# Context products moved into the attention stage, a first tile turned early, and fewer barriers in a two-layer decoder kernel

## What is computed

```
k = concat(context, x) ; q = x @ wq ; scores = q . (k @ wk) / sqrt(D)
out = softmax(scores) @ (concat(context, x) @ wv) @ wo
```

## Time and profile before

| what | us |
|---|---|
| median of 3 runs | 2226.31 (2226.2 to 2229.31) |
| the profiled execution's own time | 2224.11 |
| its span in the trace | 2222.4 |
| PE busy | 2093.0 (94%) |
| DVE busy | 1250.0 (56%) |
| POOL busy | 541.8 (24%) |
| ACT busy | 516.3 (23%) |

### The profile page before, as it was taken

One profiled execution on the slowest core, in us unless ns is written; L12 is line 12 of the kernel. 1 busy time (PEld: TensorE's weight loads), 2 busy tenths in 40 slices (PEclk: granted clock), 3 DMA queues, 4 the chain that ended last, 5 costly groups with the idle time before them and its releaser, 6 DMA issues. The chain is left out here.

```text
span 2222.4 us, 29341 instructions
## 1 busy us (share of the span) xinstructions
PE 2093.0 (94%) x11935; PEld 1221.2 (55%) x11935; DVE 1250.0 (56%) x1825; ACT 516.3 (23%) x783; POOL 541.8 (24%) x511
## 2 busy tenths in 40 slices
PE   7899999878999899899999898999999999999996
PEld 5444444324444466556665565566666666666654
DVE  2467777666999944022222225365757585847466
ACT  1444444440000121111111121122222222222121
POOL 2122222226777400011111221112121212111111
PEclk9999999989999999999999999999999999999998
DMA  8950000005111145521212412101010101000000
GB/s 171 99 48 29 29 29 20 31 10 200 46 42 42 34 140 190 200 67 62 67 67 67 178 40 96 48 1 48 1 58 1 58 1 39 1 29 11 1 10 20
DMA packets 65649, 129.57 MB, mean 58 GB/s; under 512 B 6416, under 2 KB 19856, under 8 KB 65520
## 3 DMA queue, kind: packets, MB, share of 16 engines
q1 hardware_dynamic: 44864, 75.39, 13.3%
q10 hardware_dynamic: 14976, 33.69, 4.2%
q0 software_dynamic: 5680, 18.62, 2.8%
HBM read 96.36 MB, written 41.81 MB: 62 GB/s over the span
## 5 line engine op out<-in xcount | busy, mean ns | idle before, releaser
L937 PE MATMUL conv_conv<-kv,toep 128*128 128x512 f32 x576 | 248.5, 594 | 0.0
L2434 DVE RECIPROCAL tail_inv<-tail_ring 128x256 f32<-128x256 f32 x64 | 112.4, 1756 | 188.7 <-PE tail_ring L1772 181.4
L1456 PE MATMUL moe_gu_ps<-gu,moe_xT 128*128 x624 | 199.0, 462 | 3.9 <-issue 2.3
L937 PEld LDWEIGHTS conv_conv<-kv,toep 128*128 128x128 f32 x576 | 110.0, 191 | 139.0 <-issue 131.6
L960 POOL TENSOR_TENSOR kv<-vT,cT 128x512 f32<-128x512 f32 x128 | 147.2, 1172 | 58.1 <-PE conv_conv L937 53.6
L1456 PEld LDWEIGHTS moe_gu_ps<-gu,moe_xT 128*128 128x128 f32 x624 | 116.0, 191 | 73.0 <-issue 23.6
L2125 POOL TENSOR_TENSOR tail_rstd_x<-tail_rstd_x,const_minus_half 128x2 f32<-128x2 f32 x31 | 21.9, 707 | 499.0 <-DVE tail_rstd_x L2386 499.0
L2132 POOL TENSOR_SCALAR_AFFINE_SELECT tail_expT<-tail_expT 128x1024 f32<-128x1024 f32 x64 | 71.2, 1112 | 237.3 <-ACT tail_expT L2207 237.1
L543 POOL TENSOR_SCALAR_AFFINE_SELECT front_expT<-front_expT 128x2048 f32<-128x2048 f32 x32 | 64.4, 2012 | 256.1 <-ACT front_expT L599 256.1
L1540 DVE TENSOR_TENSOR moe_hid<-moe_gu_ps,moe_silu 128x352 f32<-128x352 f32 x39 | 20.4, 524 | 179.3 <-PE moe_gu_ps L1456 179.3
L599 ACT ACTIVATE front_expT<-front_scores 128x2048 f32<-128x2048 f32 x48 | 90.1, 1878 | 81.1 <-PE front_scores L354 81.1
(11 more groups left out here) (372 smaller groups left out, 4006.0 us busy)
## 6 DMA issues: line engine op xcount, KB each, us to landing
toep<-toeplitz SPq DMA_DIRECT2D x32, 320.0 KB, 2.9
y_slots<-moe_y ACTq DMA_DIRECT2D x39, 256.0 KB, 2.0
gu<-in_L_ffn_gate_up_proj SPq DMA_DIRECT2D x5, 1408.0 KB, 11.2
toeplitz<-filt_rows SPq DMA_DIRECT2D x1, 6144.0 KB, 66.7
front_e<-in_ctx SPq DMA_DIRECT2D x8, 512.0 KB, 5.5
toeplitz<-filt_rows SPq DMA_DIRECT2D x2, 2048.0 KB, 88.5
x_after<-x SPq DMA_DIRECT2D x8, 512.0 KB, 5.1
tail_x<-x_after SPq DMA_DIRECT2D x8, 512.0 KB, 4.0
```

The costliest lines, as they stand in the source:

```text
L937: ins = pe.matmul(bank, toep[p][:, mat * P:(mat + 1) * P], kv[p][:, c].rearrange("p b j i -> p (b j i)"), start=n == 0, stop=n == len(PART ...
L1456: ins = pe.matmul(gu_ps[:, s % 2, h, 0:HID], xT[:, c, :], wgu[c][:, e, h * HID:(h + 1) * HID], start=c == 0, stop=c == NC - 1)
L2434: link.after(dve.reciprocal(inv[c % 2][:], bank[:, S:2 * S]))
```

## The change

1. `ctx_values` of batches 0, 1 and 2 (`EARLY = 3`) go from the routing stage into the last three rounds of the attention stage, between scores and behind the turned context; the output weights are loaded over `wq`, the results are drained by ACT into buffers that are free by then, and stored.
2. In every round `turn_context` is split into two halves, one ahead of the third score; ACT does `squares(a, 0)` ahead of `take_sums(a, 1, 0)`, and POOL `add_eps(a, 0)` ahead of `causal(a, 5)`.
3. `ctx_queries(0)` goes between the turned `wk` and the turned `wv`. The store of the context queries is issued ahead of the context values.
4. The first tile of the experts is turned in the routing stage, ahead of the last `ctx_values`, and copied by DVE there.
5. The wait for the stored expert rows goes from ACT's end of the expert stage to POOL's start of the tail; the constants, the kept tiles and the middle's semaphores are given back without a barrier of their own, the last after the tail.
6. In the tail the third batch is turned ahead of the second batch's output rows.

```diff
@@ retire @@
-        self.nc.all_engine_barrier()
+        if not self.lasts:
+            self.nc.all_engine_barrier()
@@ front_stage, tensor @@
+                def ctx_values(b, t, parts=(0, 1)):
+                    key = ("ctxo", b, t)
+                    if 0 in parts:
+                        pe.wait_ge(ctx_wo_loaded, 16)
+                        ring.claim(pe, key)
+                    for c in range(NC // 2 * parts[0], NC // 2 * (parts[-1] + 1)):
+                        ins = pe.matmul(ring.tile(key), cT[:, b, c, t * P:(t + 1) * P], wide["wq"][:, c, :], start=c == 0, stop=c == NC - 1,
+                                        skip_group_check=True)
+                    if 1 in parts:
+                        ins.then_inc(ring.filled_sem(key), 1)
...
                         score(a, 0)
+                        if a == B - 1: ctx_values(0, 0, (0,))
                         if f is not None: square_sums(f, 0)
+                        if a == B - 1: ctx_values(0, 0, (1,))
...
                         score(a, 1)
-                        if f is not None: weigh(f, 1, 1, ("O",))
+                        if f is not None:
+                            weigh(f, 1, 1, ("O",))
+                            turn_context(f, 0)
...
                             weigh(f, 1, 1, ("Z",))
-                            turn_context(f)
+                            turn_context(f, 1)
...
                         if u is not None: turn_tokens(u)
+                        if a == B - 1: ctx_values(0, 1, (0,))
                         score(a, 4)
...
                         if f is not None: square_sums(f, 1)
+                        if a == B - 1: ctx_values(0, 1, (1,))
                         score(a, 5)
+                        if a == B - 1: ctx_values(1, 0)
...
                     elif f is not None:
-                        turn_context(f)
+                        for n in range(2):
+                            turn_context(f, n)
+                        ctx_values(1, 1)
                         weigh(f, 1, 1)
                         square_sums(f, 0)
                         turn_tokens(u)
+                        ctx_values(2, 0)
                         square_sums(f, 1)
                         octets(u)
                         for t in range(NT):
                             out(f, t)
+                        ctx_values(2, 1)
@@ front_stage, sync @@
+                        key = ("q", B - 1, 3)
+                        sp.wait_ge(ring.filled_sem(key), ring.count(key))
+                        sp.dma_start(wide["wq"][:], ctx_wo.rearrange("(c p) e -> p c e", p=P)).then_inc(ctx_wo_loaded, 16)
@@ front_stage, gpsimd @@
+                        add_eps(a, 0)
                         causal(a, 5)
-                        add_eps(a, 0)
@@ front_stage, scalar @@
+                def take_ctx_values(b, t):
+                    rows = (xT, qT[0])[b % 2]
+                    if b >= 2 and t == 0:
+                        act.wait_ge(ctx_o_stored[b % 2], 16 * (b // 2))
+                    take(("ctxo", b, t), pair(rows, t))
+                    if t == 1:
+                        for n in range(NT):
+                            key = ("ctxo", b, n)
+                            act.wait_ge(ring.drained_sem(key), ring.count(key))
+                        act.dma_start(ctx_o[b].rearrange("p t d -> p (t d)"),
+                                      rows[:].rearrange("p c s -> p (c s)")).then_inc(ctx_o_stored[b % 2], 16)
...
                             take(("ctx", f, n), cT[:, f, 2 * n:2 * n + 2, :])
+                        take_ctx_values(1, 1)
                         take_sums(f, 1, 1)
                     if f is not None: root(f, 0)
                     if a is None and u is not None:
                         for n in range(2):
                             take(("x1", u, n), vT[:, 2 * n:2 * n + 2, u, :])
+                    if a is None and f is not None: take_ctx_values(2, 0)
+                    if a == B - 1: take_ctx_values(0, 0)
...
+                            take(("ctx", f, 0), cT[:, f, 0:2, :])
                             take_sums(f, 1, 1)
-                            for n in range(2):
-                                take(("ctx", f, n), cT[:, f, 2 * n:2 * n + 2, :])
+                            take(("ctx", f, 1), cT[:, f, 2:4, :])
                         squares(f, 1)
...
                         act.activation(warm[:], half[:, 0:1], ACT.Exp)
+                        if a == B - 1:
+                            take_ctx_values(0, 1)
+                            take_ctx_values(1, 0)
+                        elif a is None:
+                            take_ctx_values(2, 1)
...
                         exps(a, 5)
+                        squares(a, 0)
                         take_sums(a, 1, 0)
-                        squares(a, 0)
@@ middle_stage, tensor @@
                 natural("wk")
+                for c in range(NC):
+                    drained(("natural", "wq", c))
+                ctx_queries(0)
                 natural("wv")
...
-                ctx_queries(0)
-                ctx_values(0)
+                ctx_queries(1)
                 pe.wait_ge(shaped, 1)
                 pe.wait_ge(picks_ready, 1)
...
-                for b in range(1, B - 2):
+                for b in range(2, B - 2):
                     ctx_queries(b)
-                    ctx_values(b)
-                    if b == 2:
+                    if b == B - 3:
+                        pe.wait_ge(mid.gathered[0], 16)
+                        bank = ring.claim(pe, "tile")
+                        for c in range(NC):
+                            ins = pe.transpose(bank[:, c * P:(c + 1) * P], mid.xg[0][:, c * P:(c + 1) * P], consts["ident"][:])
+                        ins.then_inc(ring.filled_sem("tile"), 1)
+                    if b >= EARLY:
+                        ctx_values(b)
+                    if b == EARLY:
                         pe.wait_ge(hot_ready, 1)
@@ experts_stage @@
-                turn_x(0)
                 pe.wait_ge(mid.first_half, 16 * 7)
                 gate(0)
...
                 store(TILES - 1)
-                for p in range(2):
-                    act.wait_ge(y_stored[p], 16 * len(range(p, TILES, 2)))
@@ tail_stage @@
                 weigh("P", 1, 3)
+                turn("P", "x3", 2)
                 for n in range(NC):
                     drained(("P", "W", 1, n))
...
+                for p in range(2):
+                    pool.wait_ge(y_stored[p], 16 * len(range(p, TILES, 2)))
                 fetch(0)
```

More of the change, by code:

```diff
@@ L282, in drained, with turn @@
                     pe.wait_ge(ring.drained_sem(key), ring.count(key))
-                def turn(name, b, rows):
-                    for a in range(2):
+                def turn(name, b, rows, halves=(0, 1)):
+                    for a in halves:
                         bank = ring.claim(pe, (name, b, a))
@@ L403, in turn_tokens, with turn_context @@
                     turn("x1", u, x[u % NX])
-                def turn_context(f):
+                def turn_context(f, half):
                     pe.wait_ge(e_loaded[f % NE], 16 * (f // NE) + 16)
-                    turn("ctx", f, e[f % NE])
+                    turn("ctx", f, e[f % NE], (half,))
                 pe.wait_ge(constants_made, 7)
@@ L865, in __init__ @@
         self.ctx_stored = [st.sem(f"ctx_stored{p}") for p in range(2)]
+        self.y_stored = [st.sem(f"y_stored{p}") for p in range(2)]
+        self.early_stored = [st.sem(f"early_stored{p}") for p in range(2)]
         self.gathered = [st.sem(f"gathered{p}") for p in range(2)]
@@ L1030, in _, with ctx_stores @@
                             sums(h, lc, 1)
+def ctx_stores(b):
+    return sum(2 if n >= EARLY else 1 for n in range(b % 2, b, 2))
 def middle_stage(nc, consts, mid, region, base, x_out, vT, cT, w_router, w_gu, w_down, wa, wvo, ctx_q, ctx_o, slot, share):
@@ L1269, in take_ctx @@
                     if b >= 2:
[L1270 removed]
+                        act.wait_ge(mid.ctx_stored[p], 16 * ctx_stores(b))
                     for j in range(2):
                         take(("ctxq", b, j), ctxq[p][:, 2 * j:2 * j + 2, :].rearrange("p c s -> p (c s)"))
+                    for j in range(2):
+                        key = ("ctxq", b, j)
+                        act.wait_ge(ring.drained_sem(key), ring.count(key))
+                    act.dma_start(ctx_q[b], ctxq[p][:]).then_inc(mid.ctx_stored[p], 16)
+                    if b < EARLY:
+                        return
                     for t in range(NT):
                         take(("ctxo", b, t), ctxo[p][:, t, :])
[L1275 removed]
+                    for t in range(NT):
+                        key = ("ctxo", b, t)
                         act.wait_ge(ring.drained_sem(key), ring.count(key))
[L1277 removed]
                     act.dma_start(ctx_o[b], ctxo[p][:]).then_inc(mid.ctx_stored[p], 16)
@@ L1291, in _ @@
                 load_down(act, w_down, mid.down, 0, lo, half, mid.first_half)
```

(14 more changed lines are left out.)

46 lines of the change are left out of this document (24 added, 22 removed).

## The result

The change makes the kernel faster: 2209.7 us (median of 4 runs, 2207.43 to 2210.99) against 2227.74 us (4 runs, 2226.2 to 2229.31); ratio 0.9916, 95% interval 0.9901 to 0.9932. The profiled execution took 2208.73 us (span 2206.8) against 2224.11, so 15.4 us less where the working had 22.2. The time lies inside the range (2194 to 2212), near its upper end: 5.7 us above the point.

A forecast was written before the change was run, and what follows sets the result against it. PE (TensorE) was taken to bound the kernel nearly everywhere, 94% busy over the span. The terms summed to -22.2 us, from 2224.11 to 2201.9, or 2204 as a median; range 2194 to 2212.

The forecast's parts named there:

- Routing stage: Three context value products leave (-20.6), context queries 0 move to its head (-1.7), the first tile's transposes enter (+0.5).
- First tile: Start of the expert stage: it begins with its gate product, and the second gate comes only 2 us sooner: -1.9.
- store waits: Start of the tail: less idle time for PE (-2.1) and half the first queries' lower-clock time regained (1.0): -3.1.
- third batch: Tail: turning the third batch during PE's 4.67 us wait for DVE saves 1.8 us (0 if DVE's norm were late).
- Last two rounds: End of the attention stage: early products mostly hidden in the last scores' round (-1.6); delayed weighing and squares after it (+5.1).
- Steady rounds: Six attention rounds: POOL's mask holds DVE, delaying the second score; loss 0.75 us a round, +4.5 in all.
- L725 near 2 us in every round: Steady attention rounds: sign of a right forecast, this DVE operation held by POOL's mask, its median before being 0.478 us.
- A: Rival: in the steady rounds DVE isn't held by the mask and the swap wins, 6 x 1.55 better: 2195 us; chance 0.19.
- B: Rival: second held operation (+4.5), last round's low clock longer, barriers worth nothing: 2212 us; chance 0.15 with D's mild form.
- C: Rival: early products not hidden in the last two attention rounds; six whole products cost 20.6 us: 2221 us; chance 0.06.
- D: Rival: first tile's gather lands late behind 6 MB of weights: 2211 us, or slower than before from 46 us; proper chance 0.02.
- Holding or sharing: Steady rounds: whether POOL's instruction holds DVE's operation to its end (+0.75 a round, taken) or shares (about 0.1 a round).

The follow-up runs named there:

- e2: Changed kernel with only ACT's order undone (copies the sums before it squares), POOL still adding eps before its mask: 2192.22 us, ratio 0.985 to the kernel before.
- e4: Changed kernel with ACT squaring the last batch before copying the third early product's first half, in the round after the last scores: 2204.15 us, ratio 0.9905.
- e7: Against e5, the last batch is weighed before the second half of batch 1's context product, in the round after the last scores: 2193.24 us, ratio 0.985.
- e1: Changed kernel with the steady rounds' swap undone on both ACT and POOL: 2195.72 us, ratio 0.9862 to the kernel before.
- e5: Changed kernel with the edits of both e2 and e4: 2191.36 us, ratio 0.9838 to the kernel before.
- e12: e5 with two matmuls of the tail's last context value product made twice, ahead of a PE wait: 2187.99 us, ratio 0.9827 to the kernel before.
- e10: Kernel before the change with only the swap of the two pairs on ACT and POOL: 2239.16 us, ratio 1.0056.
- e8: Against e5, each half of the early context products keeps only its first of four matmuls: 2192.65 us, ratio 0.985 to the kernel before.
- e3: Changed kernel with only POOL's order undone (mask before adding eps), ACT still squaring before it copies the sums: 2198.25 us, ratio 0.988 to the kernel before.
- e9: Changed kernel with the first query product of each steady round made twice, filling PE's wait before the second score: 2202.86 us, ratio 0.9893 to the kernel before.
- e11: Changed kernel with two matmuls of the tail's last context value product made twice, ahead of a PE wait: 2205.14 us, ratio 0.9907 to the kernel before.

## Why the prediction was right, and where it was off

- *Routing stage.* Right: -21.8 in the ledger, with the forecast -20.6, -1.7 and +0.5 (6.9 less 5.3 is 1.6, where the sum has 1.7). The first turn of rows moved by 5.45 us (forecast 5.3), and the token product had no idle remark, at a margin of 0.3 us between DVE's marks (876.70) and PE's coming (876.99), forecast 0.4.
- *First tile, store waits, third batch, end.* Right within 0.7 us each: -2.0, -3.8, -1.8, -0.4. The final turn and the start of the convolution gave -2.5 where the sum had -0.9: the octet products there took 1.96 instead of 3.75 us. Of the first queries of the tail the whole fall went in this execution (7.14 us; I took back half), but e2 and e4 have it (8.82 and 8.83 us) behind the same wait of 1.93 us.
- *Last two rounds.* Right: -1.2 and +5.2, and the octet products at the full clock (1.98 us). The reason for the second half of the +5.2, the squares queued behind the copy, is shown by e4. That for the first half (a bank drained late) is only part of it; e7 shows that with POOL's new order the last mask holds the weighing too (here it ends at 486.52 us, and the weighing starts at 488.33).
- *Steady rounds*: the step that failed. "Loss 0.75 a round" is what the wait costs where the clock stays, to 0.02 us (196.03 to 252.69). It was priced at the full clock, although the same text priced the clock at two other places. Counted between first scores, four of the six rounds were 2.2 to 2.3 us longer, because PE's work behind the 1.91 us ran at the lower clock; one was 0.8 us longer, one 0.9 us shorter. Together they cost 8.7 us in this execution where the term was +4.5. Of the term, 1.15 a round (6.9 us) stood for the swap and -0.4 for the halved turn. Putting the swap alone into the kernel before costs 12.4 us, undoing it in the changed one gains 15.8, so its price was too small by 5.5 to 9 us; the halved turn gave back 0.3 a round (e1's 55.6 against 55.9). The sign "L725 near 2 us in every round" did not come: L724's product was held in its place.
- *Luck.* The ledger shows +6.4 and not +8.7 because this execution came to the first of these rounds 2.4 us ahead (79.71 against 82.09 us): the products behind the landing of the weights ran 7.17 us here and 8.86 in the one of before. This isn't the change's doing (e5 has 8.86, e12 has 7.17). Without it the miss of 6.6 us in the ledger would have been 9. That the time fell within the range is owed in part to this and to the 1.6 us at the start of the convolution, which offset part of what was missed.
- *What was not in the sum*: 6.3 us of lower clock in parts of the tail that the diff doesn't touch. The sum held each wait that the change leaves alone at its old price.
- *Rivals.* A fell by e10 and e1 (the swap never wins; half of it, POOL's, does, by e2). B came nearest in size, for another reason: no second operation of DVE was held. C fell by e8, D by the landing of 8.3 us.
- *Holding or sharing.* The forecast took holding from its rows and kept the other reading at 0.1 us a round. The Trainium skill ("SBUF — State Buffer", section "SBUF: two separate sides") is plain: a GpSimd instruction that reads SBUF and a VectorE instruction with two SBUF inputs share an exclusive lock, held for the whole instruction, and the other one blocks. The trace agrees in each of four orders: 2.19 us behind the mask, 1.48 and 1.49 behind the add, 1.17 behind its rest, and no delay for the maxima, which have no two SBUF inputs.

What stays open: why one wait is followed by the lower clock and another of the same length is not. Of the two places in the tail, the one near 1333 us is not tied to the change: e2, e3, e5, e7 and e9 lack the fall, and e10, with the tail of before, has it (5.60 us). The one near 2054 us may be: the product of 2.01 us takes 3.72 or 3.73 in all twelve profiles of kernels with the changed tail and 2.01 in both with the tail of before (the kernel before and e10), though nothing near it was changed. No run undid the turned third batch or the moved store waits, so which of them, if any, brings it wasn't tried.

## What to carry to other kernels

Price an idle time of PE twice: once as the wait, once as what PE's next matmuls cost at the lower of the two clock levels; here the second was nearly twice the first, and it came and went without the instructions changing. Work that fills a wait can be worth more than its own time, and taking it out can gain nothing. Before swapping two instructions of POOL, look at which of DVE's two-input SBUF operations will meet the longer one.

## What the runs showed of the hardware that was not expected

- A 1.9 us idle time of PE was followed by matmuls at the lower level: a score of 1.14 us became 1.21 to 2.09, a weighing of 1.92 became 2.50 to 3.49. The fall came behind 4 of 5 such waits in one execution, behind 6 of 6 in another of the same program, and behind 2 of 6 (e4) and 3 of 6 (e11, one of its waits 1.64 us) in two that have the same instructions up to there.
- 8 useless matmuls in each steady round made the kernel 7 to 9 us faster (2202.86 against 2209.7 and 2211.5 us, beside different runs of the kernel before; the ratios to the kernel before are 0.9893 against 0.9916 and 0.9929), and about 15 us of matmuls less did not make it faster (2192.65 against 2191.36 us).
- A DVE operation with two SBUF inputs that met a POOL instruction ended 0.28 us after it, whichever it was: 254.77 behind 254.49 (the mask, changed kernel), 249.66 behind 249.38 and 247.62 behind 247.34 (the add, e1 and e2), 248.46 behind 248.18 (its rest, e3). The hold works both ways: POOL's mask took 2.19 us instead of 2.01 where it was issued while DVE's product was still running (e2, 247.30 us).
